# A gated cross-attention and memory kernel: an order of its own for the last token tile

## The reference

```python
a   = softmax((LN(x) @ Wq.T + bq) @ (ctx @ Wk.T + bk).T / sqrt(2048)) @ ctx
x1  = x + tanh(g_xattn) * a
h   = LN(x1)                                   # needs mean and variance of each row of x1
q   = h @ fWq.T                                # 64 columns
top = top_k((q @ Wr.T) @ (aux_keys @ Wr.T).T / sqrt(48) + log_rel, 8)     # of 512 slots
z   = softmax(q @ aux_keys[top].T / 8 + log_rel[top]) @ aux_values[top]
lv  = log1p(var(h))
u   = clip(0.5 * lv / (mean(lv) + 1e-6) + 2.5 * sigmoid(gelu(h @ Wu1.T + bu1) @ Wu2.T + bu2), 0, 5)
gate = sigmoid(gate_w1 * clip((u - 0.5) / 1.5, 0, 1) + gate_bias)         # 0 where below 0.05
out = x1 + tanh(g_ffn) * (h + gate * (z @ Wvd.T @ Wvu.T))
```

## Time and profile before

| what | value |
|---|---|
| median of 3 runs | 1095.2 us (1094.51 to 1099.56) |
| the profiled execution | 1094.26 us |
| its span | 1092.5 us |
| TensorE busy | 1053.9 us (96%) |
| VectorE, ScalarE, GpSimd busy | 768.6, 552.8, 182.7 us |
| DMA | 218.90 MB, 200 GB/s in the mean |

### The profile page before, as it was taken

The page is one execution under the profiler, slowest core; times in us unless marked ns, Lnnn a source line. Parts: engine busy times, 40 slices in busy tenths (PEclk is TensorE's granted clock), DMA queues, the critical chain, the costliest instruction groups (busy, mean ns, idle before and its releaser), DMA issues. The chain is left out here.

```text
span 1092.5 us, 19631 instructions
## 1 busy us (share of the span) xinstructions
PE 1053.9 (96%) x6890; PEld 1009.0 (92%) x6890; DVE 768.6 (70%) x1844; ACT 552.8 (51%) x860; POOL 182.7 (17%) x351
## 2 busy tenths in 40 slices
PE   6999999999998999999999999999999994999997
PEld 6999999998998999999999999999999994888886
DVE  6655546456746877777777778776877766788785
ACT  3333477654625454545454545454554543555643
POOL 0610000000002222222223131312222322000000
PEclk9999999999999999999999999999999996999999
DMA  7433646689449982744343744437353517999999
GB/s 280 145 134 135 236 175 253 265 285 280 130 144 233 233 227 79 191 134 123 107 117 113 201 124 109 121 102 212 100 142 82 149 39 226 392 389 400 404 422 382
DMA packets 106588, 218.90 MB, mean 200 GB/s; under 512 B 48052, under 2 KB 64468, under 8 KB 91608
## 3 DMA queue, kind: packets, MB, share of 16 engines
q1 hardware_dynamic: 96760, 180.68, 53.3%
q10 hardware_dynamic: 9216, 33.56, 7.9%
q0 software_dynamic: 576, 4.19, 0.9%
HBM read 174.10 MB, written 54.79 MB: 210 GB/s over the span
## 5 line engine op out<-in xcount | busy, mean ns | idle before, releaser
L56 PE MATMUL tk_bank<-b_weights,k_turned 128*128 128x384 f32 (+2 forms) x1088 | 359.4, 330 | 3.3 <-DVE k_turned L1334 1.6
L58 PE MATMUL tk_bank<-b_weights,k_turned 128*128 128x384 f32 (+2 forms) x1088 | 350.2, 322 | 0.0
L57 PE MATMUL tk_bank<-b_weights,k_turned 128*128 128x384 f32 (+2 forms) x1088 | 350.1, 322 | 0.0
L56 PEld LDWEIGHTS tk_bank<-b_weights,k_turned 128*128 128x128 f32 x1088 | 205.0, 188 | 7.4 <-issue 3.1
L57 PEld LDWEIGHTS tk_bank<-b_weights,k_turned 128*128 128x128 f32 x1088 | 205.2, 189 | 1.3
L58 PEld LDWEIGHTS tk_bank<-b_weights,k_turned 128*128 128x128 f32 x1088 | 204.6, 188 | 0.0
L1325 DVE STREAM_TRANSPOSE tk_bank<-k_rows 128x512 f32<-128x512 f32 x128 | 133.4, 1066 | 7.4 <-DMA k_rows<-in_x_dram 7.1
L1137 ACT ACTIVATE k_turned<-tk_bank 128x512 fp32r<-128x512 f32 x128 | 73.7, 595 | 82.2 <-DVE tk_bank L1325 75.1
L1334 DVE TENSOR_TENSOR k_turned<-tk_bank,k_turned 128x512 fp32r<-128x512 f32 x128 | 82.7, 685 | 8.0 <-ACT k_turned L1137 6.8
L1700 DVE TENSOR_TENSOR late_x<-late_x,ob_out 128x512 f32<-128x512 f32 x96 | 65.7, 687 | 23.9 <-PE ob_out L58 22.6
L56 PE MATMUL tk_bank<-k_turned,a_T 128*128 128x256 f32 x256 | 77.3, 302 | 0.5 <-DVE a_T L254 0.5
(11 more groups left out here) (229 smaller groups left out, 2199.8 us busy)
## 6 DMA issues: line engine op xcount, KB each, us to landing
k_rows<-in_x_dram SPq DMA_DIRECT2D x40, 1024.0 KB, 4.9
k_rows<-in_x_dram SPq DMA_DIRECT2D x128, 256.0 KB, 5.2
late_x<-in_x_dram SPq DMA_DIRECT2D x24, 1024.0 KB, 8.4
out_dram<-late_x ACTq DMA_DIRECT2D x48, 512.0 KB, 14.2
k_rows<-in_Wk_dram SPq DMA_DIRECT2D x16, 1024.0 KB, 4.8
k_rows<-in_Wq_dram SPq DMA_DIRECT2D x16, 1024.0 KB, 4.9
out_dram<-k_rows ACTq DMA_DIRECT2D x16, 512.0 KB, 11.5
b_weights<-scratch_b SPq DMA_DIRECT2D x6, 1024.0 KB, 8.0
```

The costliest lines, as they stand in the source:

```text
L56: pe.matmul(out, lh, rh, start=start, stop=False, skip_group_check=skip)
L57: pe.matmul(out, lh, rl, start=False, stop=False, skip_group_check=skip)
L58: return pe.matmul(out, ll, rh, start=False, stop=stop, skip_group_check=skip)
```

## The change

The last tile gets code of its own on every engine. TensorE (`last_tile`) forms the cw products of psB already after half of the a-chunks, under a semaphore of their own (`cov_sum`); tile 31's query and routing stand between its last a-chunks, and the psA half with `c_sum` comes behind them. VectorE takes the variance on `cov_sum`, starts the gates' arrays behind tile 31's query, and takes over `inner` and the sum; `scales` and tile 31's `hw` go to GpSimd; ScalarE takes the logarithm before the context's copy. The statistics that `kept_stats` tells of are three without the learned value, which goes straight into the kept array. SyncE loads batch 0's context after `b_sum` (the b-chunks) and only x after `c_sum`.

```diff
@@ sync
-            sp.wait_ge(S["c_sum"], TILES)
+            sp.wait_ge(S["b_sum"], TILES)
             sp.wait_ge(keep["ctx_stored"], 16)
             load_ctx(sp, scr, keep, 0)
+            sp.wait_ge(S["c_sum"], TILES)
             for t in range(2 * W_SLOTS):
...
@@ tensor
+            def last_tile(t, u):
...
+                late_z(t - 2)
+                late_route(t - 1)
+                a_part(t, u, 0, False)
...
+                pe.transpose(att_turned_ps, att2[u], ident[:]).then_inc(S["att_turned"], 1)
+                a_part(t, u, 1, False)
...
+                for weights_in, stop in ((cw1, False), (cw2, True)):
+                    ins = pe.matmul(psB[u][:, NCTX:BW], attS[:], weights_in[:, 0:CWN - UB], start=False, stop=stop,
+                                    skip_group_check=True)
+                ins.then_inc(S["cov_sum"], 1)
+                a_part(t, u, 2, False)
+                late_turn_w(t - 1)
+                late_query(t)
+                a_chunks(u, range(12, 14))
+                late_route(t)
+                a_chunks(u, range(14, 16))
...
+                ins.then_inc(S["c_sum"], 1)
+                late_z(t - 1)
+                late_turn_w(t)
+                pe.wait_ge(S["log_summed"], 1)
+                pe.matmul(ps_total[:, 0:1], keep["ones"][:], rowsum, start=True, stop=True).then_inc(S["all_summed"], 1)
+                late_z(t, last=True)
@@ scalar
             late_w_out(t - 1)
-            late_square(t)
             late_q_hi(t)
-            late_tanh(t)
-
-            context_high(act, keep, keep["ctx_hi"], 0)
             act.wait_ge(S["ready"], 1)
             act.activation(v["log"], v["one_plus"], ACT.Ln).then_inc(S["logged"], 1)
+            context_high(act, keep, keep["ctx_hi"], 0)
             late_exp(t)
+            late_square(t)
+            late_w_out(t)
+            late_tanh(t)
@@ gpsimd
            tile(TILES - 1, 1, last=True)
-            late(TILES - 1, 1)
-            late_keep(TILES - 1, 1)
...
+            power(st2[u][:, 2:3], st2[u][:, 1:2], ve[:]).then_inc(S["rstd2"], 1)
+            pool.drain()
+            pool.wait_ge(S["query"], t + 1)
+            pool.tensor_copy(keep["stats"][:, t, 0:3], st2[u][:, 0:3]).then_inc(S["kept_stats"], 1)
+            pool.drain()
+            scales()
+            pool.wait_ge(S["hidden"], t + 1)
+            pool.tensor_tensor(hw, hid, keep["wu2"][:], ALU.mult).then_inc(S["hw"], 1)
@@ vector
+            late_stats(t - 1, 1 - u, BATCH - 1, False)
+            late_scale(t - 1, 1 - u)
             dve.wait_ge(keep["wvu_hi"], 1)
             dve.tensor_tensor(keep["wvu_out"][1], f32(keep["wvu_out"][1]), f32(keep["wvu_out"][0]),
                               ALU.subtract).then_inc(keep["wvu_lo"], 1)
...
+            late_slots(t - 1)
+            att_lo(t)
+            late_learned(t - 1, 1 - u)
+            late_stats(t, u, BATCH - 1, False, last=True)
+            last_query(t, u)
+            gates_begin()
             late_q_lo(t)
+            late_z_scale(t - 1)
+            gates_ratio()
+            late_slots(t)
+            last_hidden(t, u)
+            late_z_out(t - 1)
+            gates_log()
             late_poly(t)
-            late_z(t - 1)
-            late_learned(t, u)
-            gates_begin()
-            late_slots(t)
+            last_learned(t)
             gates(t)
```

More of the change, by code:

```diff
@@ L963, in prepare_and_token_block @@
         mean, var, rstd, learned = (keep["stats"][:, :, k] for k in range(4))
-        v = {n: hw[:, k * TILES:(k + 1) * TILES] for k, n in enumerate(names)}
-        total, rowsum, half_bu2 = (hw[:, len(names) * TILES + k:len(names) * TILES + k + 1] for k in range(3))
+        small = rest[:, 3 * P + 4 * NCTX:]
+        v = {n: small[:, k * TILES:(k + 1) * TILES] for k, n in enumerate(names)}
+        total, rowsum, half_bu2 = (small[:, len(names) * TILES + k:len(names) * TILES + k + 1] for k in range(3))
         ps_total = psA
@@ L1036, in a_part, with a_chunks @@
                     pe.wait_ge(S["hidden"], t)
-                for c in range(4 * g, 4 * g + 4):
+                a_chunks(u, range(4 * g, 4 * g + 4))
+            def a_chunks(u, chunks):
+                for c in chunks:
                     split_product(pe, psA[:, 0:UB], (xT[u][0][:, c, :], xT[u][1][:, c, :]),
@@ L1118, in _ @@
                 tile(2 + u, u, j=1)
-            with pe.Fori(2, PAIRS) as j:
+            with pe.Fori(2, PAIRS - 1) as j:
                 for u in range(2):
                     tile(2 * j + u, u, j=j)
[L1122 to L1129, removed]
+            tile(TILES - 2, 0, j=PAIRS - 1)
+            last_tile(TILES - 1, 1)
         @block.scalar
@@ L1362, in att_lo, with late_stats @@
                                   ALU.subtract).then_inc(S["att_lo"], 1)
-            def late_stats(t, u, batch, first):
-                dve.wait_ge(S["c_sum"], t + 1)
+            def late_stats(t, u, batch, first, last=False):
+                if last:
+                    dve.wait_ge(S["cov_sum"], 1)
+                else:
+                    dve.wait_ge(S["c_sum"], t + 1)
                 if not first:
@@ L1385, in late_scale, with last_query, last_hidden, last_learned @@
                                          ALU.add).then_inc(S["hidden"], 1)
+            def last_query(t, u):
+                dve.wait_ge(S["rstd2"], t + 1)
+                dve.tensor_scalar(q2[:, 0:BOT], psB[u][:, QC:QC + BOT], st2[u][:, 2:3], None, ALU.mult)
+                dve.tensor_scalar(q2[:, BOT:2 * BOT], psB[u][:, QC:QC + BOT], st2[u][:, 2:3], None,
+                                  ALU.mult).then_inc(S["query"], 1)
+                dve.scalar_tensor_tensor(hid[:, 0:UA], psB[u][:, QC + BOT:BW], st2[u][:, 2:3], keep["bu1"][:, 0:UA],
+                                         ALU.mult, ALU.add)
+            def last_hidden(t, u):
+                dve.wait_ge(S["c_sum"], t + 1)
+                dve.scalar_tensor_tensor(hid[:, UA:HU], psA[:, 0:UB], st2[u][:, 2:3], keep["bu1"][:, UA:HU], ALU.mult,
+                                         ALU.add).then_inc(S["hidden"], 1)
+            def last_learned(t):
+                dve.drain()
+                dve.tensor_tensor(act1, act1, hid, ALU.mult).then_inc(S["inner"], 1)
+                total_of_all()
+                dve.wait_ge(S["tanh"], t + 1)
+                dve.wait_ge(S["hw"], t + 1)
+                dve.scalar_tensor_tensor(act1, act1, 1.0, hw, ALU.add, ALU.mult,
+                                         accum_out=keep["stats"][:, t, 3:4]).then_inc(S["learned"], 1)
             def late_q_lo(t):
@@ L1463, in gates @@
                 op(dve.reciprocal, total, total)
-                op(dve.tensor_scalar, v["log"], v["log"], total, 0.5, ALU.mult, ALU.mult)
+                dve.tensor_scalar(v["log"], v["log"], total, 0.5, ALU.mult, ALU.mult)
+            def gates(t):
                 dve.wait_ge(S["unit"], 1)
```

61 lines of the change are left out of this document (45 added, 16 removed).

## The result

The changed kernel takes **1090.91 us** in the median of 10 runs (1088.79 to 1093.46), the kernel before, run beside it, 1095.74 (10 runs). The ratio is 0.9946, with a 95% interval from 0.9932 to 0.996: 0.54% less time, with an interval clear of 1. The forecast was 1091.7. The profiled execution took 1089.61 us, its span is 1087.8, 4.7 shorter than before.

What follows compares the result with a forecast made beforehand. Two lines bound the end: the small-step chain then TensorE (6.7 us earlier), and the transfer stream (3.0 us earlier), taken as deciding. 1094.26 - 3.0 = 1091.3, from the median 1092.2; middle 1091.7 us, range 1087.2 to 1095.2.

Steps and rivals of the forecast that it cites:

- the step that chose the number: Output block: the transfer stream ends 3.0 us earlier and sets the end, although TensorE could be 6.7 us earlier.
- Line 1, the chain: Small steps on VectorE and ScalarE before the output block: selection starts 7.3 us earlier, gates and block start 6.7 us earlier.
- The wait for the split: TensorE, before tile 31's routing: ready at 905.65, it waits 0.8 us for VectorE's split of the query.
- Line 2, the transfers: DMA stream from `c_sum` on: `c_sum` 2.2 us later, but the context already out, so the stream is 3.0 us ahead.
- the first late load: Output block, near tile 29: TensorE's earlier start turns into longer stores and a first x load arriving late.
- rival A: Output block: TensorE alone sets the end, 6.7 us earlier, 1087.6 us, up to 1088.5; chance 0.18.
- B: Output block: stores crowd out the loads and TensorE waits; gain 0 to 1.5 us, about 1094; chance 0.14 with D.
- C: Tile 31's query split holds TensorE and delays `c_sum`, with GpSimd's copy blocked 2.19 us: about 1096 us; chance 0.08.
- D: Gates don't start earlier because the learned sum is late; 6 us more would undo line 1; chance 0.14 with B.
- The DMA share stays 1.0: Sign for the forecast in the output block, to the end; a share below 1 with over 5 us saved meant A.
- The stores' landings are longer than before: Sign for the forecast in the output block: stores take longer to land than in the kernel before.
- some of ScalarE's passes over x are released by a load: Sign for the forecast in the output block: some passes wait for an x load, where VectorE's addition released them before.

Runs made afterwards that it cites:

- Run 1: The kernel before, with only batch 0's context loaded after `b_sum` as in the change, so x lands earlier: 1096.56 us against 1096.79, ratio 0.9998.
- run 7: The changed kernel with both contexts after `b_sum`, four x loads after `cov_sum` and two after `c_sum`: 1090.34 us against 1096.19 for the kernel before, ratio 0.9938.
- run 5: The changed kernel with TensorE's last a-products and context products ahead of tile 31's query and routing, no overlap: 1094.06 us against 1096.81 before, ratio 0.9979.
- Run 4: The changed kernel with the six x loads held back until the logarithms' sum: 1093.35 us against 1096.79 for the kernel before, ratio 0.9967.
- run 10: Early transfers and 48 extra products on the changed kernel, plus routing behind `c_sum`, hidden layer before selection, polynomial behind it, ScalarE's square before its exponential: 1088.56 us, ratio 0.9925.
- run 6: The changed kernel with tile 31's routing behind `c_sum` instead of between the last a-chunks: 1089.89 us against 1096.19 for the kernel before, ratio 0.9938.
- run 8: The changed kernel with 48 extra unused products of 320 columns in TensorE's idle time: 1089.84 us against 1096.19 for the kernel before, ratio 0.9941.
- run 9: The changed kernel with both the earlier x and context transfers and the 48 extra TensorE products: 1088.58 us against 1096.19 for the kernel before, ratio 0.9928.
- run 11: The kernel of run 10 with GpSimd's product `hw` waiting for the selection's end: 1088.81 us against 1096.81 for the kernel before, ratio 0.9936.
- run 12: The kernel of run 10 with 24 instead of 30 extra products behind the last z product: 1087.32 us against 1097.2 for the kernel before, ratio 0.9911.

## Why the prediction came out right

**The time** was 0.8 us from the forecast, and most of the way there was right, but not the step that chose the number. Part of the 0.8 is luck: the forecast took 3.5 us (0.32%) off the 1095.2 of the kernel before, which measured 1095.74 beside the changed one, and the measured ratio takes 0.54% off, with 0.4% as its lower end. The saving was forecast too small.

*Line 1, the chain* holds to a few tenths. Variance 902.7, measured 902.26; the query's turn 904.6, measured 904.58; routing 906.45, measured 906.07; selection 908.1, measured 907.92; its end 911.25, measured 911.00; gates' end 919.2, measured 919.47; block 920.3, measured 920.54. The wait for the split was 0.17 us instead of 0.8, and from the selection's end to the gates' end it took 8.5 us instead of 8.0. One row explains that: the pair of array operations at 911.70 took 1.0 us more beside `hw`. The forecast had seen such a loss, 0.5 us, elsewhere, between `scales` and the first gate arrays, and had left it out of its sum. Those ran side by side from 904.15 to 906.44, and VectorE's arrays took 1.32 us there (904.37 to 905.69) against 1.23 before.

*Line 2, the transfers* was right in its sizes: `c_sum` by 909.05, the first x load issued at 908.70; landed 914.0, measured 913.5. What failed is the sentence after it, "the stream's part behind that first tile has the same bytes and the same share of 1.0. It ends 3.0 us earlier", and the choice made on it, "I take the value at the stream because its share never leaves 1.0". Run 1 gives the stream its lead and gains nothing; run 7 gives it 3.0 us more and gains nothing that can be measured; run 5 moves the start back and the stream ahead, and the time goes with the start. A DMA share of 1.0 says that the DMA engines have work all the time. It doesn't say that anyone waits for it: every load of x had landed at least 2.6 us before its pass, and only SyncE waits for the stores' long landings. 4.98 against 4.86 us a tile is a debt of 4 us in 32 tiles, and it was paid from the loads' lead over their passes. That falls from 18.3 us (tile 7) to 2.6 (tile 29), before from 20.0 to 2.8; the first late load that the forecast saw near tile 29 didn't come. Run 4, with the stream 6.0 us later, shows where that ends. The rows by which the forecast measured the debt were a poor choice, too: the store at 943 with its 4.7 us was the fastest of all 64.

*So rival A was the mechanism*, with the price it was given too high: 6.7 us, where 4.8 came. Its start was right to 0.3; the missing term is the clock. In the changed kernel the clock was at its upper level until 918.2, fell 2.3 us before the block, and came back 7.9 us into it instead of 5.1. The forecast had the row for it, 0.50 in the block's first stretch, and took the block's length as fixed. With 1.6 us for it, A's 1087.6 becomes 1089.2, against 1089.61. The forecast came near because 3.0 lies near 4.8: its reason for 3.0 was wrong.

*Rivals B, C and D* did not come: no load was late, TensorE waited 0.17 us for the split, the learned sum was in time. C's GpSimd row did repeat in another place, without a consequence:

```profile
890.98 3.27 POOL L1312 TENSOR_TENSOR k_rows<-k_rows,c_wu 128x512 f32<-128x512 f32 x1 [1.37 <-DVE k_rows L1445]
```

Tile 30's `hw` takes 3.27 us beside VectorE's 2048-column product, against 1.27 for tile 31's at 911.61: 2.0 more, where the forecast had 2.2 by the 2.19 of the earlier trace rows. The Trainium skill (SBUF — State Buffer, on the shared port pair) says that a VectorE instruction with both inputs in SBUF and a GpSimd one that reads SBUF exclude each other. These two rows agree, and so does the pair at 911.70. In run 10 `hw` ran at full speed beside MAX8 and MATCH_REPLACE8, which read `tk_bank`, a bank that TensorE writes. So it depends on which instruction VectorE runs; that the inputs decide is argued, not tried.

*Signs named in advance*: transpose, variance, x load and context came where they were said to. "The DMA share stays 1.0" came, but it couldn't tell the two lines apart: it was to fall below 1 under rival A, and A was the mechanism. "The stores' landings are longer than before" didn't come (median 13.5 us against 13.7), nor did "some of ScalarE's passes over x are released by a load", and that last one was the sign that told the two lines apart.

*Still open*: the last store's landing, 3.4 to 7.4 us over the runs. It was 3.8 with x early, but 5.3 with x early and TensorE busy, so no rule can be read from it, and with single profiles of it none of the differences under 0.3% between runs 6 to 9 can be explained.

## What to carry to other kernels

A saturated resource is the bound only if somebody waits for it late: before taking a busy share for a limit, look for the wait row that ends on it, and move the two candidates apart in an experiment (here an earlier stream with an old chain). When a chain is shortened ahead of a stretch on TensorE, price the stretch's own first microseconds anew: the clock at its start was not the same after another order of work ahead of it, and here that took back a quarter of the gain. And where an engine's queue is reordered, list the transfers that its instructions wait for: one of them moved ahead (the context on ScalarE) turns a hidden load into 9 us of standing still.

## What the runs showed of the hardware

- The same block took 157.6 to 160.5 us (run 4 aside) with the granted clock of its first 8 us: 1.00 throughout in runs 9 and 10 (157.6 and 157.7), 0.50 for 3.4 us in runs 8, 11 and 12 (159.1 to 159.2), 0.50 for its first 5.1 us in the kernel before (158.9) and for its first 7.9 us in the changed one (160.5). Runs 8 to 11 all had 48 small products in TensorE's idle time, so these alone don't decide it.
- A row of GpSimd can be 2.6 times as long beside a large VectorE product (3.27 us against 1.27) and VectorE's 32-column pair 3.3 times as long beside GpSimd's (1.49 against 0.45), while the first two steps of the selection on VectorE are not changed by the same neighbour (3.08 us for the whole in the changed kernel and in run 10).
- In the changed kernel a stream at a DMA share of 1.01 to 1.02 and 397 to 420 GB/s, from 927 to 1080, let stores land after up to 20.3 us, and no pass waited for a load.
